# Token stage of an audio block: values folded into one mixing matrix, x loaded behind its last reader

## The reference

```python
xv = x.reshape(n, b, t, d).transpose(1, 0, 3, 2)
q = jnp.einsum('bndt,st->bnds', xv, Wq) + bq
kv = jnp.einsum('bndt,st->bnds', xv, Wkv) + kv_bias      # kv_bias is zero for k
k = kv[:, :, :, 0, :]; v = kv[:, :, :, 1, :]              # after a reshape
q = q * scale
attn = jax.nn.softmax(jnp.einsum('bnds,bndr->bnsr', q, k), axis=-1)
out = q.transpose(0, 1, 3, 2) + jnp.einsum('bnsr,bndr->bnsd', attn, v)
...
h = _L0_tok_ref(x, ...)
h = h + _L0_attn_ref(_layernorm(h, axis=-1), ...)
h = h + _L0_ffn_ref(_layernorm(h, axis=-1), ...)
```

## Time and profile before

| | us |
|---|---|
| median of 3 runs | 993.04 |
| range of the runs | 992.38 to 993.05 |
| span of the profiled execution | 994.2 |
| PE busy | 962.1 |
| DVE busy | 815.9 |
| ACT busy | 680.0 |
| POOL busy | 655.9 |

### The profile page before, as it was taken

The page is one execution under the profiler, slowest core; times in us unless marked ns, Lnnn a source line. Parts: engine busy times, 40 slices in busy tenths (PEclk is TensorE's granted clock), DMA queues, the critical chain, the costliest instruction groups (busy, mean ns, idle before and its releaser), DMA issues.

```text
span 994.2 us, 25841 instructions
## 1 busy us (share of the span) xinstructions
PE 962.1 (97%) x7402; PEld 831.6 (84%) x7402; DVE 815.9 (82%) x1997; ACT 680.0 (68%) x2469; POOL 655.9 (66%) x936
## 2 busy tenths in 40 slices
PE   7889999999999999999999999999999999999988
PEld 4778888898888898888898888888888888888877
DVE  4788888888888888888888888888888888888862
ACT  3557677667777667777667767666767666867653
POOL 2677666777666767666767666767666677766670
PEclk9999999999999999999999999999999999999999
DMA  6044554444554444545444545444445444445330
GB/s 192 23 128 107 146 145 125 123 126 114 149 141 133 115 132 111 153 135 141 112 134 112 144 135 145 114 132 117 136 135 149 114 131 120 131 135 153 97 108 22
DMA packets 193633, 124.56 MB, mean 125 GB/s; under 512 B 31185, under 2 KB 185169, under 8 KB 193617
## 3 DMA queue, kind: packets, MB, share of 16 engines
q1 hardware_dynamic: 190880, 120.98, 44.3%
q10 hardware_dynamic: 2736, 3.38, 1.0%
HBM read 69.26 MB, written 55.05 MB: 125 GB/s over the span
## 4 chain that ended last, share of the span: by engine, by line
PE 65%; DMA 16%; DVE 6%; SPq 6%; issue 3%; POOL 2%; ACT 1%; DVEq 0%; POOLq 0%
PE ring L846 14%; PE ring L1061 13%; PE ring L917 8%; DMA ET<-spill 8%; DMA spill<-EB 8%; PE ring L824 6%; SPq L253 5%; PE ring L884 5%; PE bank L865 5%; PE ring L985 3%; DVE EB L596 2%; PE ring L994 2%; PE bank L994 2%; PE bank L1028 2%; PE ring L981 1%
## 5 line engine op out<-in xcount | busy, mean ns | idle before, releaser
L330 ACT ACTIVATE E<-ring,m_neg 128x128 f32<-128x128 f32 x768 | 273.2, 380 | 19.2 <-DVE m_neg L582 18.2
L468 POOL TENSOR_TENSOR qkT<-rot_c,rot_s 128x256 f32<-128x256 f32 x256 | 187.3, 732 | 20.1
L476 POOL TENSOR_TENSOR E<-E,e_rcp 128x512 f32<-128x512 f32 x158 | 175.2, 1124 | 37.0 <-DVE e_rcp L605 37.0
L330 ACT ACTIVATION_READ_ACCUMULATOR E<-ring,m_neg 128x1 f32 x768 | 166.8, 217 | 0.0
L466 POOL TENSOR_TENSOR rot_s<-rot_s,rope_qs 128x256 f32<-128x256 f32 x192 | 146.5, 763 | 2.8 <-DVE rot_s L570 2.4
L865 PE MATMUL bank<-wout_sb,G 128*128 128x192 f32 x744 | 141.1, 326 | 0.0
L582 DVE TENSOR_REDUCE m_neg<-ring 128x4 f32<-128x512 f32 x192 | 129.9, 678 | 9.8 <-PE ring L884 9.8
L596 DVE STREAM_TRANSPOSE EB<-E 128x512 f32<-128x512 f32 x186 | 124.9, 687 | 15.1 <-POOL E L476 15.1
L1061 PE MATMUL ring<-wo_sb,OT 128*128 128x192 f32 x744 | 133.5, 329 | 0.5 <-DVE OT L627 0.4
L1061 PEld LDWEIGHTS ring<-wo_sb,OT 128*128 128x128 f32 x744 | 119.4, 190 | 7.4 <-issue 7.4
L865 PEld LDWEIGHTS bank<-wout_sb,G 128*128 128x128 f32 x744 | 119.7, 190 | 0.4 <-issue 0.4
(11 more groups left out here) (159 smaller groups left out, 2486.3 us busy)
## 6 DMA issues: line engine op xcount, KB each, us to landing
spill<-EB SPq DMA_DIRECT2D x186, 256.0 KB, 2.3
ET<-spill SPq DMA_DIRECT2D x248, 128.0 KB, 2.8
ET<-spill SPq DMA_DIRECT2D x248, 64.0 KB, 2.3
x_sb<-in_x_dram SPq DMA_DIRECT2D x64, 192.0 KB, 2.5
out_dram<-out_sb SPq DMA_DIRECT2D x62, 96.0 KB, 2.3
x_sb<-in_x_dram SPq DMA_DIRECT2D x64, 64.0 KB, 2.4
w_raw<-in_w_att_dram ACTq DMA_DIRECT2D x2, 608.0 KB, 5.0
win_raw<-in_w_in_dram ACTq DMA_DIRECT2D x2, 384.0 KB, 6.3
```

What stands on the lines that cost most here:

```text
L330: last = nc.scalar.activation(E[:, a, s * P:(s + 1) * P], RING[a][:, s * P:(s + 1) * P], ACT.Exp, bias=m_neg[:, a, s:s + 1], accum_out=e_s ...
L468: nc.gpsimd.tensor_tensor(qkT[:, b, :, a], rot_c[:, b, :, a], rot_s[:, b, :, a], ALU.add).then_inc(q_out, 1)
L476: nc.gpsimd.tensor_tensor(e, e, r, ALU.mult).then_inc(prob_out, 1)
```

## The change

Since `out = (attn Wv + scale Wq) x` but for the biases, one matrix per sequence is made and applied to x. Values and second queries are no longer computed. DVE turns `t_a` itself (`tok_turned`, in blocks of 32 by 32, enough since attention stays within groups of 8 rows), PE multiplies it with a block-diagonal Wv (`tok_mix`, 256 columns), DVE adds Wq on the way out of PSUM (`tok_mixed`, to `t_m`), and PE applies it to x (`tok_h`, four matmuls of 64 output rows and 192 columns in place of two of 128 output rows). `h_next` is then a plain copy, and ACT makes it. The bias of a row is a constant over its features, which the layer norm takes out again; so it goes only into the copies kept for the residual sum: POOL multiplies `t_a` with the bias row (`token_bias`), ACT sums it and adds it (`residual_kept`). The copy of the attention's v out of PSUM moves from DVE to ACT. The rows of h are no longer swapped by halves, so a result is stored with one DMA and not with two. `tok_h` is now the last reader of x, so `load_ahead` waits for it; from pass 2 on it stands behind ten more matmul instructions of `ffn_second`.

```diff
             def load_ahead(n):
-                sp.wait_ge(s_mm, n)
+                sp.wait_ge(h_mm, n)
                 load(n)
...
             def store(n):
                 sp.wait_ge(res_out, n + 1)
-                for k in range(2):
-                    sp.dma_start(out[bass.ds(2 * n, 2), k * D2:(k + 1) * D2].rearrange("a r d -> r a d"),
-                                 out_sb[(1 - k) * D2:(2 - k) * D2]).then_inc(stored, 16)
+                sp.dma_start(out[bass.ds(2 * n, 2)].rearrange("a r d -> r a d"), out_sb[:]).then_inc(stored, 16)
...
-                def tok_vq(i):
-                    act.wait_ge(vq_mm, 2 * n + i + 1)
-                    for k, (dst, bias) in enumerate(((t_v, bias_rows[:, 1:2]), (t_q, bias_sc[:]))):
-                        r0 = (i ^ k) * (P // 2)
-                        rows = slice(r0, r0 + P // 2)
-                        nc.scalar.activation(dst[rows], TOK_VQ[i][rows].rearrange("p (a d) -> p a d", a=2),
-                                             ACT.Identity, bias=bias[rows]).then_inc(vq_out, 1)
+                def v_out_of_psum():
+                    need(act, pv_mm, 4 * (p - 1) + 2)
+                    act.wait_ge(v_mm, p + 1)
+                    nc.scalar.copy(v_tok[:], V_MM[:, :, V_OF:DP]).then_inc(v_out, 1)
+
+                def h_added():
+                    act.wait_ge(h_mm, n + 1)
+                    need(act, xn_out, 2 * n)
+                    nc.scalar.copy(h_next[:], TOK_H.rearrange("p (a d) -> p a d", a=2)).then_inc(h_out, 1)
+
+                def residual_kept():
+                    act.wait_ge(bias_out, p + 1)
+                    for a in range(2):
+                        nc.scalar.activation(t_d[:, a], t_c[:, a], ACT.Identity,
+                                             accum_out=t_bias[:, a:a + 1]).then_inc(bias_sum, 1)
+                    act.wait_ge(h_out, p + 1)
+                    need(act, h2_out, 2 * p - 1)
+                    act.wait_ge(bias_sum, 2 * p + 2)
+                    nc.scalar.activation(h_cur[0][:], h_next[:, 0, :], ACT.Identity,
+                                         bias=t_bias[:, 0:1]).then_inc(h_kept[0], 1)
+                    nc.scalar.activation(h_wait[:], h_next[:, 1, :], ACT.Identity,
+                                         bias=t_bias[:, 1:2]).then_inc(h_moved, 1)
...
-                if tok:
-                    act.wait_ge(aT_mm, n + 1)
-                    nc.scalar.copy(t_aT[:].rearrange("p a c -> p (a c)"), TOK_AT).then_inc(aT_out, 1)
+                if tok and not att:
+                    h_added()
                 if att_first:
                     score_exp(0, 1)
+                    h_added()
...
                     act.wait_ge(h_moved, p + 1)
                     need(act, h2_out, 2 * p)
                     nc.scalar.copy(h_cur[1][:], h_wait[:]).then_inc(h_kept[1], 1)
+                if tok and att and not att_first:
+                    h_added()
...
+                def token_bias():
+                    if isinstance(p, int) and p == -1:
+                        pool.wait_ge(s_scaled, 5)
+                    pool.wait_ge(t_norm, n + 1)
+                    need(pool, bias_sum, 2 * n)
+                    nc.gpsimd.tensor_tensor(t_c[:], t_a[:], bias_qv[:].rearrange("p (o c) -> p o c", o=1).broadcast_to([P, 2, P]),
+                                            ALU.mult).then_inc(bias_out, 1)
...
-                def h_added():
-                    dve.wait_ge(h_mm, n + 1)
-                    need(dve, h_moved, n)
-                    nc.vector.tensor_tensor(h_next[:], TOK_H.rearrange("p (a d) -> p a d", a=2), t_q[:],
-                                            ALU.add).then_inc(h_out, 1)
+                def tok_turned():
+                    dve.wait_ge(t_norm, n + 1)
+                    need(dve, m_mm, n)
+                    nc.vector.transpose(t_aT[:].rearrange("p a (j c) -> p a j c", j=NB),
+                                        t_a[:].rearrange("p a (j r) -> p a j r", j=NB)).then_inc(aT_out, 1)
+
+                def tok_mixed():
+                    dve.wait_ge(m_mm, n + 1)
+                    need(dve, h_mm, n)
+                    nc.vector.tensor_tensor(t_m[:].rearrange("p a i s -> p (a i) s"),
+                                            TOK_M.rearrange("p (x s) -> p x s", x=4),
+                                            bd_qk[:, 0:P // 2].rearrange("p (o s) -> p o s", o=1).broadcast_to([P, 4, P // 2]),
+                                            ALU.add).then_inc(m_out, 1)
...
-                if att:
-                    v_out_of_psum()
...
+                if tok:
+                    tok_turned()
+                    if isinstance(p, int) and p == -1:
+                        tok_mixed()
                 if ffn and att:
-                    heads_out(p - 1)
+                    heads_out(p - 1, (0,))
                 if att:
                     key_max(0, (2,))
+                if ffn and att:
+                    heads_out(p - 1, (1,))
+                if att:
                     sums_inverted(0, 0, p)
...
@@ -743,6 +778,8 @@
                 elif att:
                     sums_inverted(0, 1, p)
                     normalised(0, p)
+                    if tok:
+                        tok_mixed()
                 if ffn:
                     dve.wait_ge(h_kept[1], p)
                     attention_added(1, 2 * p)
...
                     normalise(h2, mv2, rs2, hn, 1).then_inc(hn_out[1], 1)
-                if tok and not att_first:
-                    h_added()
...
-                def tok_vq():
-
-                    need(pe, h2_out, 2 * p - 1)
-                    if first == "tok":
-                        pe.wait_ge(s_bd, 5)
-                    for i, bank in enumerate(TOK_VQ):
-                        nc.tensor.matmul(bank, bd_vqv[:, i:i + 2].rearrange("p b c -> p (b c)"),
-                                         x_sb[:, i].rearrange("p a d -> p (a d)"), start=True, stop=True).then_inc(vq_mm, 1)
-
...
-                def tok_probs_turned():
+                def tok_mix():
                     if first == "tok":
-                        pe.wait_ge(s_const, 16 * 6)
-                    pe.wait_ge(t_norm, n + 1)
-                    for a in range(2):
-                        last = nc.tensor.transpose(TOK_AT[:, a * P:(a + 1) * P], t_a[:, a, :], ident[:])
-                    last.then_inc(aT_mm, 1)
+                        pe.wait_ge(s_bd, 3)
+                    need(pe, XL_out, n)
+                    pe.wait_ge(aT_out, n + 1)
+                    nc.tensor.matmul(TOK_M, bd_v[:], t_aT[:].rearrange("p a c -> p (a c)"),
+                                     start=True, stop=True).then_inc(m_mm, 1)
 
                 def tok_h():
                     if att:
                         pe.wait_ge(exp_out, 6 * p + 1)
-                    pe.wait_ge(aT_out, n + 1)
+                    pe.wait_ge(m_out, n + 1)
                     for a in range(2):
-                        last = nc.tensor.matmul(TOK_H[:, a * D:(a + 1) * D], t_aT[:, a, :], t_v[:, a, :],
-                                                start=True, stop=True)
+                        for i in range(2):
+                            last = nc.tensor.matmul(TOK_H[i * (P // 2):(i + 1) * (P // 2), a * D:(a + 1) * D], t_m[:, a, i],
+                                                    x_sb[:, i, a], start=True, stop=True)
                     last.then_inc(h_mm, 1)
...
-                if tok:
-                    tok_vq()
...
-                if tok:
-                    tok_probs_turned()
                 if fin:
                     ffn_second(0, p - 2, range(2, 4))
+                if tok:
+                    if first == "tok":
+                        pe.wait_ge(s_const, 16 * 6)
+                    tok_mix()
                 if ffn and not ends:
                     output(1, p - 1)
-                if tok:
+                if tok and not fin:
                     tok_h()
                 if first == "tok":
                     kept_warm(4)
@@ -1106,6 +1133,8 @@
                 if fin:
                     ffn_second(0, p - 2, range(4, NM))
                     ffn_second(1, p - 2, range(3))
+                    if tok:
+                        tok_h()
```

108 lines of the change are left out of this document (55 added, 53 removed).

## The result

The changed kernel takes 1169.18 us (median; 1165.90 to 1172.42), the kernel before 993.04 us (992.38 to 994.86) beside it. The ratio is 1.1768, with an interval of 1.1749 to 1.1786: slower by 176 us. The forecast of 1119 us had the direction and the mechanism; the time lies 19 us above the upper end of its range.

A forecast was written before the change was run, and what follows sets the result against it. Bound: PE's waits at `probs_v(0)`, for the way over DVE, SP and DMAs, and level with DVE at `tok_scores`. 28 x (3.5 + 0.9) + 2.7 makes 126 us on 994.2, 1120.1; median 1119 us, range 1085 to 1150.

The forecast's parts named there:

- `tok_h` paired: Half-width matmuls of `tok_h` run side by side on PE's two halves: 0.7 us, or 1.3 if not.
- PE the bound: Rival: PE's net saving of 1.15 us a pass counts in full, 957 us; chance 0.04.
- The hold: On SP's queue, x waits for `tok_h` and delays the spills of sequence 0: +3.5 us in each pass.
- everything after it keeps its distances: From the delayed first spill to the refills and `probs_v(0)`, spacing stays as before, giving +3.5 us a pass.
- upper bound: Delay of the spills at most 4.6 us: `tok_h` unpaired (+0.6), spill sharing DMAs with x (+0.5).
- The clock: PE idles about 3.0 us ahead of `probs_v(0)` and its granted clock falls: 0.9 us a pass, between 0 and 1.7.
- part of the low stretch is spent waiting: Some low-clock time lies in PE's wait ahead of `probs_v(0)`; a reason for 0.9 us a pass.
- one fall costs at most 1.7 us: A 3.4 us stretch at 1.2 GHz doubles PE's work time, so a fall costs at most 3.4 / 2 us.
- the clock falls in every pass: Rival: PE's clock falls each pass, 28 x 5.2 + 2.7 us, 1141 us; chance 0.17, shared with no pairing.
- The third rival: The load of x is no hindrance; only DVE's 0.7 us counts, in 30 passes: about 1013 us, chance 0.05.
- DVE's 0.7 us being contained in it: DVE's later sum and turned blocks, 0.7 us, lie within the 3.5 us delay of the spills and add nothing.
- start, pass 1 and pass 30: Outside the 28 passes: +1.0 us at the start, +1.0 in pass 1, +0.7 in pass 30, together 2.7 us.

The follow-up runs named there:

- e1: The changed kernel with SP's load of x issued behind the spills and refills of sequence 0: 1013.58 us, ratio 1.0185.
- e2: The changed kernel with five matmuls on zeros on PE ahead of `probs_v(0)`, the load still held: 1120.67 us, ratio 1.127.
- f2: The changed kernel with x loaded behind the refills, and `tok_mixed` and `tok_h` moved behind attention work: 1013.21 us, ratio 1.0207.
- e3: The kernel before, old token stage, with `tok_h` behind the feed-forward's ten matmul instructions and x's load waiting for it: 1143.62 us, ratio 1.1491.

## Why the prediction was right and wrong

**Direction and mechanism: right; two sizes: wrong.** The changed kernel waits on the queue, and the wait is where the prediction put it: x behind `tok_h`, the first spill 2.34 us behind the first x issue (forecast 2.2), PE idle ahead of `probs_v(0)` (3.86 us, forecast 3.0). A pass takes 35.6 us, above the 33 to 35 that were named. `tok_h` paired. The wins of the change were none, as worked out: `tok_vq`'s 1.3 us became a wait of 1.0 to 1.2 us for `kT2` in each pass. The rival "PE the bound" is out.

**The hold: 4.2 us instead of 3.5.** The step "everything after it keeps its distances" failed by half of this: the spill and its landing ahead of ET took 3.66 us instead of 3.33, with 512 KB of x under way on the same DMAs. The chain shows it, changed kernel:

```profile
536.00 3.07 DMA spill<-EB
```

The row before had 2.68; in e1, where x comes later, spill to ET is back at 3.34. Every run agrees: over the 28 passes the second piece of the spill landed 3.11 to 3.18 us behind its issue in the four kernels that issue x just ahead of it, and 2.69 to 2.76 in the ten others. The prediction had this (+0.5) in its upper bound and left it out of the sum. The rest is the way to `tok_h`, 10.21 us behind `tok_scores` instead of 10.06, and the four issues, 2.37 us instead of 2.2.

**The clock: 1.7 us instead of 0.9.** This is the larger of the two errors: 22 us over 28 passes, the hold 20. Either alone would have left the time inside the range (1141 or 1139 us); together they make 1161. The step that failed is "part of the low stretch is spent waiting", by which the term was halved. The clock falls late in the gap: at 542.6 of a wait that ends at 543.56. So nearly the whole low stretch lies over work (4.4 of 4.9 us on average), it comes in every pass, and in 12 of 28 it is 6.8 us long. From a stretch of 3.4 us in the trace of before, "one fall costs at most 1.7 us" was taken for the upper bound: the measured mean happens to be 1.7, but it is a mean of short and long stretches, and no bound. Nor did the clock of before fall only once: it fell again at 39.4, behind gaps of 1.07 and 0.73 us with two transposes between them, again for 3.4 us. The window (us, length, busy, granted clock, DMA share, GB/s), kernel before:

```profile
39.00:43.00 4.00, 3.51 (x30) 0.57 0.00 0
```

Two falls behind such short gaps spoke rather for a fall in each pass. The rival "the clock falls in every pass", at 1.7, was the right case; it had a chance of 0.17, and its 1141 us were still 28 too low. The Trainium skill (TensorE: Matmul & The Clock Gate, "HAM oscillation — how this bites in real kernels") says that a wait for DMA between bursts throttles PE anew in each round; the trace agrees, with 28 falls in 28 passes, and e2 shows the counterpart, a clock of 1.00 in all 28 when the same wait is filled with matmuls. I had called the rule undecided for want of such a gap in the loop; the one gap without a fall, 1.60 us, was half as long and should have weighed less.

**The token stage alone: 0.5 us a pass, and 1013.6 us.** The third rival said 1013 us for a kernel whose load is no hindrance, by DVE's 0.7 us in 30 passes. e1 makes that kernel and takes 1013.58. That the numbers meet is luck: 14 of its 19 us lie in the 28 passes and 4 ahead of them, where the rival had 21 in the passes, and its cause was not the one given: taking `tok_mixed` away from DVE there gained nothing (f2). What the runs showed is the pair of ways told above. (`tok_turned` was put at 0.35 us from a reading of 0.6 us for 512 columns; that row says 0.69, and it took 0.43.) This term was not added to the hold in the sum, as "DVE's 0.7 us being contained in it"; the sum of e3 and e1 says that it comes on top with at least part of its size (28 x 0.75 us between the changed kernel and e3).

**The rest.** From the forecast span of 1120.1 to the profiled 1163.6 are 43.5 us: clock 28 x 0.8 = 22.4, hold 28 x 0.7 = 19.6, start, pass 1 and pass 30 with 4.2 instead of 2.7, 1.5. And the runs' median lies 5.6 us above this profiled span, where I had taken 1.2 below it from the kernel before: the profiled execution was the fastest of four (1165.90 us) and its span is 2.3 us below its own time.

## What to carry to other kernels

A DMA queue runs in the order in which it is written: before moving a load behind a later reader, list what is queued behind it and when that is due, and if the load itself is in no hurry put it last (here that is worth 156 us, and costs nothing in the kernel before). Price a new gap on TensorE of the length seen here (2.5 us and more in each pass) at its length plus the work that then runs at half the clock, in every pass, and do not count the wait as cover: here the fall came in its last 1.4 us or behind it. And work taken from one engine is a gain only if it stands on the way that ends last; here 1.3 us of matmuls became a wait, and when that was filled it became the next wait.
